# A cross-attention, attention and mixture-of-experts layer on one core: a sixth gate/up product ahead of the gate, and twelve split down products

## The chip, the cores and the metric

One core of a Trainium2 chip. The time is device microseconds of the whole program, from one launch. The profile is of one execution; its engines are TensorE (PE, with its weight loads as PEld), VectorE (DVE), ScalarE (ACT), GpSimd (POOL) and SyncE (SP), which issues the transfers.

## What is computed

The input x is 4 x 32 rows of 256 (T = 128 tokens, which fill the 128 partitions). Three blocks follow one another, each on a layer norm of x and added to x:

```
x = x + xattn(layernorm(x), ctx_512)        # 16 heads, causal, keys from ctx[:, :32] (causal mask)
x = x + attn(layernorm(x))                  # 16 heads, each projection with a LoRA of rank 16
x = x + ffn(layernorm(x))

def ffn(flat):                              # D = 256, I = 128, E = 32 experts, K = 4
    scores = sqrt(softplus(flat @ router_w.T))
    idx = top_k(scores + expert_bias, 4);  p = normalised scores of these, else 0
    for each expert e:
        g = clip(flat @ gate_w[e].T, -7, 7);  u = clip(flat @ up_w[e].T, -7, 7)
        out += p[:, e] * ((silu(g) * u) @ down_w[e].T)
    out += the same with a shared expert, without p
```

All 32 experts are computed for all 128 tokens; the gate p is zero for most.

## The kernel before

Each engine has its own list of instructions, written out by hand, and runs it in order; semaphores tie the lists together (`wait_ge`, `then_inc`). Nothing is reordered by a scheduler, so the place of an instruction in its list matters.

**Units.** The experts are worked on in PAIRS = 16 pairs. Pair index p counts from 0; unit n = p + 1 is the work on it, and unit 0 is the shared expert. A unit goes through these steps:

- TensorE, `gate_up(n)` (L580): the gate and up products of both experts into one PSUM bank of 512 columns.
- VectorE, `clip(n)` (L957 on): bank to `gu_clip`.
- ScalarE, `silu_unit(n)` (L785): SiLU of the gate halves, written back into the bank.
- VectorE, `gate_h(n)` (L1010): SiLU times up times routing weight, into `h`.
- TensorE, `transpose_h(n)` (L596): h is transposed into a PSUM bank (`bHT`, two in turn).
- ScalarE, `hT_unit(n)` (L793): bank to `hT` or `hT_parts`. For split downs VectorE, `hT_low(n)` (L1029), subtracts to get the low half.
- TensorE, `down(n)` (L608): the down product, added up in bank bY.

**Split weights.** The weights come from memory as 32-bit floats into `gu_raw` (RAW = 8 slots) and `dn_w`. A product on them as they are is a slow one. So weights are split in a rounded high part and a low part, and three faster matmuls (high x high, high x low, low x high) take the place of one. For pairs 2 to 15, ScalarE writes the high part of the gate/up weights (`gu_high`, `gu_high_chunk` for a half, L693 and L700) and GpSimd the low one (`gu_low`, two tiles of 128 x 512 per pair), into `gu_w` with SLOTS = 7 slots. The cast of pair p >= 9 waits until the product whose slot it overwrites is done (`gu_ready`): that of pair 9 for the third product. The first WHOLE = 2 pairs are multiplied whole. The last LAST = 11 down products are split in the same way: `dn_high(i)` on ScalarE, `dn_low(i)` on GpSimd (one tile each), the first FIRST = 5 are whole. From i = 3 on the split down weights lie in slots of `gu_w` that gate/up products have left.

**Orders.** GpSimd: the low halves of pairs 2 to 15 in order, with the inverse root of the third variance ahead of pair 7, a down tile after each of pairs 12 to 15, then the remaining down tiles. TensorE: products 1 (with the shared expert and the logits in between) to 5, transposes 0 and 1, then for n = 2 to 16 product n + 4, transpose n, down n - 2, and the last two downs. The last down goes to a bank of its own (`bLast`) and waits for the last GpSimd tile. There are five banks for products (`bGU`), so product n waits for the gating of unit n - 5. VectorE: the routing, then gating 0, gating 1, clips 2 and 3, then for each n gating n, clip n + 2 and the low part of hT. ScalarE: SiLU n + 2, the cast of pair 10 + n, the copy of hT n, and the down casts due. The lines of ScalarE between the routing and the loop are these:

```
nc.scalar.activation(root[:], half_power[:], ACT.Exp, scale=0.5).then_inc(root_ready, 1)
nc.scalar.preload_act_table(ACT.Silu)
...
gu_high_chunk(WHOLE + 7, 0)
silu_unit(0)
silu_unit(1)
gu_high_chunk(WHOLE + 7, 1)
gu_high(EARLY)
silu_unit(2)
```

The end: ScalarE copies the low sums of bY (L825), VectorE adds them (L1043), then adds the last down (L1046), and the output is stored.

Of the kernel before, what the change touches and what calls it, by code (L numbers as in the profile page):

```python
# [38 lines left out]
WHOLE = 2  # L39
EARLY = 10  # L40
LAST = 11
# [18 lines left out]
def gu_slot(p):  # L60
    return (p - WHOLE) % SLOTS

# [9 lines left out]
def build(nc, x, consts, mask, small, ctx_kv, x_wq, lora, rows, attn_w, shared_w, moe_w, out):  # L72
    with ExitStack() as ctx:
# [107 lines left out]
        bGU = (bP[0][:, 0], bP[0][:, 1], bP[1][:, 0], bP[1][:, 1], bE)  # L181
# [196 lines left out]
        def _(pe):  # L378
# [196 lines left out]
            def gate_up_whole(n, k):  # L575

                return nc.tensor.matmul(bGU[n % 5][:, 0:GU], xfT[:, k, :], gu_raw[:, raw_slot(n - 1), k * GU:(k + 1) * GU],
                                        start=(k == 0), stop=(k == DC - 1))

            def gate_up(n):  # L580

                if n > 5:
                    pe.wait_ge(h_ready, n - 4)
                for k in range(DC):
                    if n <= WHOLE:
                        pe.wait_ge(ld_gu[n - 1], 16)
                        last = gate_up_whole(n, k)
                    else:
                        pe.wait_ge(gu_lo_ready[k], n - WHOLE)
                        for a, w in HI_LO:  # L590
                            last = nc.tensor.matmul(bGU[n % 5][:, 0:GU], xnT_parts[:, a, k, :],  # L591
                                                    gu_w[:, gu_slot(n - 1), w, k * GU:(k + 1) * GU],
                                                    start=(k == 0 and a == w == 0), stop=(k == DC - 1 and a == 1))
                last.then_inc(gu_ready, 1)

            def transpose_h(n, width=2):  # L596
                pe.wait_ge(h_ready, n + 1)
                if n >= 2:
                    pe.wait_ge(hT_ready, n - 1)
                if n - 2 > FIRST:  # L600
                    pe.wait_ge(hT_low_ready, n - 2 - FIRST)
                for e in range(width):
                    last = nc.tensor.transpose(bHT[n % 2][:, e * T:(e + 1) * T], h[:, n % 4, e, :], ident)  # L603
                last.then_inc(hT_psum, 1)

            def down(n):
# [8 lines left out]
                else:  # L615
# [3 lines left out]
                    if n == PAIRS:  # L619
                        pe.wait_ge(h_ready, PAIRS)  # L620
# [27 lines left out]
            for n in range(WHOLE + 1, 6):  # L648
                gate_up(n)
            transpose_h(0, width=1)  # L650
            transpose_h(1)
            for n in range(2, PAIRS + 1):
                if n + 4 <= PAIRS:
                    gate_up(n + 4)
                transpose_h(n)
                if n == 2:
                    pe.wait_ge(ln_step, 3)
                    nc.tensor.matmul(bY[:, 0:D], hT[:, 0, 0, :], shared_sb[:, DC * SHARED:], start=False, stop=False,
                                     skip_group_check=True).then_inc(y_done, 1)
                else:  # L660
                    down(n - 2)
# [4 lines left out]
        def _(act):  # L666
# [74 lines left out]
            for c in range(DC):  # L741
                gu_high_chunk(WHOLE + 2, c)
# [3 lines left out]
            gu_high(WHOLE + 3)  # L746
# [5 lines left out]
            copy_probsT(1)  # L752
            gu_high(WHOLE + 4)
# [28 lines left out]
            nc.scalar.activation(root[:], half_power[:], ACT.Exp, scale=0.5).then_inc(root_ready, 1)  # L782
            nc.scalar.preload_act_table(ACT.Silu)

            def silu_unit(n):  # L785
                act.wait_ge(clip_ready, n + 1)
                width = 2 if n else 1
                bank = bGU[n % 5] if n else bShared
                dst = bank[:, 0:width * 2 * I].rearrange("p (e w i) -> p e w i", e=width, w=2)[:, :, 0, :]
# [3 lines left out]
            def hT_unit(n, width=2):  # L793
                act.wait_ge(hT_psum, n + 1)
                dst = hT[:, n % 3, 0:width] if n <= FIRST else hT_parts[:, n % 3, 0]
                nc.scalar.activation(dst, bHT[n % 2][:, 0:width * T], ACT.Copy).then_inc(hT_ready, 1)  # L796
# [9 lines left out]
            gu_high_chunk(WHOLE + 7, 0)  # L806
            silu_unit(0)
            silu_unit(1)
            gu_high_chunk(WHOLE + 7, 1)
            gu_high(EARLY)  # L810
            silu_unit(2)
            hT_unit(0, width=1)
            for n in range(1, PAIRS + 1):
# [7 lines left out]
                for i in range(UNITS, LAST):  # L821
                    if dn_from(i) + 1 == n + 4:
# [5 lines left out]
        def _(dve):  # L828
# [126 lines left out]
            def clip(n):  # L955
                width = 2 if n else 1
                bank = bGU[n % 5] if n else bShared  # L957
# [18 lines left out]
            step(nc.vector.tensor_scalar(logits_n, bLogits, rstd[:, 2:3], None, ALU.mult))  # L976
            dve.wait_ge(one_plus_ready, 1)
# [19 lines left out]
            dve.wait_ge(zeroed, 3)  # L997
            step(nc.vector.tensor_copy(score2[:, E:E + 1], leftover[:]))
# [11 lines left out]
            def gate_h(n):  # L1010

                dve.wait_ge(silu_ready, n + 1)
                if n >= 4:
                    dve.wait_ge(hT_psum, n - 3)
                bank = bGU[n % 5] if n else bShared
                for e in range(2 if n else 1):
                    weight_e = gate[:, (n - 1) * 2 + e:(n - 1) * 2 + e + 1] if n else rstd[:, 2:3]
                    last = nc.vector.scalar_tensor_tensor(h[:, n % 4, e], gu_clip[:, n % 4, e, 1, :], weight_e,  # L1018
                                                          bank[:, e * 2 * I:e * 2 * I + I], ALU.mult, ALU.mult)
# [9 lines left out]
            def hT_low(n):  # L1029
                dve.wait_ge(hT_ready, n + 1)  # L1030
                nc.vector.tensor_tensor(hT_parts[:, n % 3, 1], bHT[n % 2][:, 0:2 * T].rearrange("p (e t) -> p e t", e=2),  # L1031
# [79 lines left out]
```

## Time and profile before

| what | us |
|---|---|
| median of three runs | 73.18 |
| the three runs | 72.33, 73.18, 77.66 |
| the profiled execution, its own time | 72.22 |
| its span, first to last instruction | 70.4 |
| TensorE busy in the span | 65.3 (93%) |
| GpSimd busy in the span | 54.2 (77%) |
| VectorE, ScalarE busy | 47.0, 46.0 |

The span is shorter than the time by what lies before the first and after the last instruction, 1.8 us here. The granted clock of TensorE was full in the whole span. Matmuls overlap one another in the records, so a group's duration is some 0.15 us longer than what it adds to the queue; in the chain of waits the overlap is taken out.

### The profile page before, as it was taken

What the parts mean: (1) busy time and instruction counts of PE and PEld (TensorE: products, weight loads), DVE (VectorE), ACT (ScalarE), POOL (GpSimd) and SP (SyncE); (2) the same over time, 40 slices, a digit from 0 to 9 for tenths busy, and PEclk for the clock granted to TensorE, in tenths of its full rate; (3) what the DMA queues carried; (4) which work ended last, traced back from release to release, by engine and by line L of the source; (5) the groups of instructions that cost most, each with busy time, mean ns of one, the idle gap of its engine ahead of it and who ended that gap; (6) DMA issues with size and microseconds to landing.
All of it is one profiled execution on the core that took longest, in us unless ns stands there. A gap on an engine that the chain in (4) does not pass through costs nothing.

```text
span 70.4 us, 1578 instructions
## 1 busy us (share of the span) xinstructions
PE 65.3 (93%) x542; PEld 48.5 (69%) x542; DVE 47.0 (67%) x133; ACT 46.0 (65%) x101; POOL 54.2 (77%) x60
## 2 busy tenths in 40 slices
PE   5999989999799999999989999999999999999940
PEld 2348647789564496467666878888887888788820
DVE  0089488486497536499999945679955887697440
ACT  0606375876998654769979899999668851275220
POOL 7430003889999996998799999999999999999000
PEclk9999999999999999999999999999999999999999
DMA  0998999999999999999999995200000000000002
GB/s 3 271 297 245 329 425 404 291 328 419 417 419 403 393 401 407 396 383 388 393 407 400 391 372 201 76 0 0 0 9 0 0 0 0 0 0 0 0 0 74
DMA packets 6343, 15.75 MB, mean 224 GB/s; under 512 B 704, under 2 KB 1472, under 8 KB 6336
## 3 DMA queue, kind: packets, MB, share of 16 engines
q1 hardware_dynamic: 6048, 15.39, 59.2%
q10 hardware_dynamic: 288, 0.27, 1.1%
q8 instruction: 4, 0.07, 0.4%
q14 instruction: 3, 0.02, 0.1%
HBM read 15.52 MB, written 0.13 MB: 222 GB/s over the span
## 4 chain that ended last, share of the span: by engine, by line
PE 52%; DMA 16%; DVE 14%; SPq 7%; ACT 4%; issue 3%; DVEq 0%; ACTq 0%
DMA gu_raw<-moe_w_dram 16%; PE bP L591 16%; PE bY L624 7%; PE bY L613 6%; PE bXT L603 5%; SPq L275 4%; PE bE L591 4%; DVE gu_clip L964 4%; PE bY L626 3%; SPq L283 2%; DVE h L1018 2%; PE bP L419 2%; PE bXT L448 1%; PE bXT L641 1%; PE bY L444 1%
## 5 line engine op out<-in xcount | busy, mean ns | idle before, releaser
L349 POOL TENSOR_TENSOR gu_w<-gu_raw,gu_w 128x512 fp32r<-128x512 f32 x27 | 33.7, 1277 | 0.6 <-ACT gu_w L705 0.6
L591 PE MATMUL bP<-gu_w,xnT_parts 128*128 128x512 f32 x66 | 18.6, 417 | 0.0
L591 PEld LDWEIGHTS bP<-gu_w,xnT_parts 128*128 128x128 f32 x66 | 12.2, 188 | 2.9 <-issue 0.5
L1018 DVE SCALAR_TENSOR_TENSOR h<-gu_clip,gate,bP 128x128 f32<-128x128 f32 x26 | 7.8, 344 | 5.2 <-ACT bP L790 5.2
L964 DVE TENSOR_SCALAR gu_clip<-bP,clip_at 128x512 f32<-128x512 f32 x13 | 10.4, 806 | 1.1 <-PE bP L591 1.1
L355 POOL TENSOR_TENSOR gu_w<-dn_w,gu_w 128x512 fp32r<-128x512 f32 x8 | 10.1, 1285 | 0.0
L698 ACT ACTIVATE gu_w<-gu_raw 128x1024 fp32r<-128x1024 f32 x9 | 9.4, 1048 | 0.3 <-issue 0.3
L796 ACT ACTIVATE hT_parts<-bXT 128x256 fp32r<-128x256 f32 x11 | 4.2, 383 | 7.1 <-PE bXT L603 7.1
L705 ACT ACTIVATE gu_w<-gu_raw 128x512 fp32r<-128x512 f32 x10 | 6.1, 621 | 1.2 <-DMA gu_raw<-moe_w_dram 1.2
L603 PE MATMUL bXT<-consts_sb,h 128*128 128x128 f32 x33 | 6.5, 277 | 0.3 <-DVE h L1018 0.2
L790 ACT ACTIVATE bP<-gu_clip,rstd 128x256 f32<-128x256 f32 x13 | 6.1, 472 | 0.4 <-DVE gu_clip L964 0.4
L603 PEld LDWEIGHTS bXT<-consts_sb,h 128*128 128x128 f32 x33 | 4.4, 140 | 2.8 <-DVE h L1018 1.2
L339 POOL TENSOR_TENSOR aw_sb<-aw_sb,lora_v 128x256 f32<-128x256 f32 x2 | 1.4, 728 | 6.3 <-DMA aw_sb<-attn_w_dram 6.3
L624 PE MATMUL bY<-gu_w,hT_parts 128*128 128x512 f32 x14 | 5.7, 433 | 0.0
L1031 DVE TENSOR_TENSOR hT_parts<-bXT,hT_parts 128x256 fp32r<-128x256 f32 x11 | 4.6, 418 | 1.0 <-ACT hT_parts L796 1.0
L455 PE MATMUL bE<-const-bfloat16-1.0 128*128 128x512 bf16 x12 | 4.5, 516 | 0.8 <-PEq L1104 0.8
L613 PE MATMUL bY<-dn_w,hT 128*128 128x256 f32 x20 | 5.1, 380 | 0.0
L591 PE MATMUL bE<-gu_w,xnT_parts 128*128 128x512 f32 x18 | 4.9, 407 | 0.0
L803 ACT ACTIVATE gu_w<-dn_w 128x512 fp32r<-128x512 f32 x8 | 4.6, 623 | 0.0
L331 POOL TENSOR_TENSOR rstd<-var_eps,inv_sqrt_power 128x1 f32<-128x1 f32 x3 | 1.8, 598 | 3.0 <-DVE var_eps L842 3.0
L626 PE MATMUL bY<-gu_w,hT_parts 128*128 128x256 f32 x14 | 3.9, 281 | 0.0
L355 POOL TENSOR_TENSOR dn_first<-dn_w,dn_first 128x512 fp32r<-128x512 f32 x3 | 3.8, 1282 | 0.0
(161 smaller groups left out, 124.8 us busy)
## 6 DMA issues: line engine op xcount, KB each, us to landing
gu_raw<-moe_w_dram SPq DMA_DIRECT2D x16, 512.0 KB, 9.6
dn_w<-moe_w_dram SPq DMA_DIRECT2D x16, 256.0 KB, 9.5
aw_sb<-attn_w_dram SPq DMA_DIRECT2D x2, 512.0 KB, 7.4
shared_sb<-shared_w_dram SPq DMA_DIRECT2D x1, 416.0 KB, 14.9
small_sb<-small_dram SPq DMA_DIRECT2D x1, 338.0 KB, 7.3
xwq_sb<-x_wq_dram SPq DMA_DIRECT2D x1, 256.0 KB, 3.5
lora_sb<-lora_dram SPq DMA_DIRECT2D x1, 256.0 KB, 4.7
ctx_sb<-ctx_kv_dram ACTq DMA_DIRECT2D x1, 192.0 KB, 3.2
```

What stands on the lines that cost most here:

```text
L349: nc.gpsimd.tensor_tensor(gu_w[:, gu_slot(p), 1, cols], gu_raw[:, raw_slot(p), cols], gu_w[:, gu_slot(p), 0, cols], ALU.subtract).then_inc ...
L355: nc.gpsimd.tensor_tensor(dn_parts(i)[:, 1], dn_w[:, at:at + 2 * D], dn_parts(i)[:, 0], ALU.subtract).then_inc(dn_lo_ready, 1)
L591: last = nc.tensor.matmul(bGU[n % 5][:, 0:GU], xnT_parts[:, a, k, :], gu_w[:, gu_slot(n - 1), w, k * GU:(k + 1) * GU], start=(k == 0 and a ...
L603: last = nc.tensor.transpose(bHT[n % 2][:, e * T:(e + 1) * T], h[:, n % 4, e, :], ident)
L613: last = nc.tensor.matmul(bY[:, 0:D], hT[:, n % 3, e, :], dn_w[:, at:at + D], start=False, stop=False, skip_group_check=True)
L624: nc.tensor.matmul(bY.rearrange("p (w n) -> p w n", w=2), hT_parts[:, n % 3, 0, e, :], parts, start=False, stop=False, skip_group_check=True)
L626: last = nc.tensor.matmul(bY[:, 0:D], hT_parts[:, n % 3, 1, e, :], parts[:, 0], start=False, stop=False, skip_group_check=True)
L698: nc.scalar.activation(gu_w[:, gu_slot(p), 0], gu_raw[:, raw_slot(p)], ACT.Copy).then_inc(gu_hi_ready, DC)
L705: nc.scalar.activation(gu_w[:, gu_slot(p), 0, cols], gu_raw[:, raw_slot(p), cols], ACT.Copy).then_inc(gu_hi_ready, 1)
L790: nc.scalar.activation(dst, gu_clip[:, n % 4, 0:width, 0, :], ACT.Silu, scale=rstd[:, 2:3]).then_inc(silu_ready, 1)
L964: nc.vector.tensor_scalar(gu_clip[:, n % 4, 0:width], bank[:, 0:width * 2 * I], clip_at[:, 0:1], clip_at[:, 1:2], ALU.min, ALU.max).then_i ...
L1018: last = nc.vector.scalar_tensor_tensor(h[:, n % 4, e], gu_clip[:, n % 4, e, 1, :], weight_e, bank[:, e * 2 * I:e * 2 * I + I], ALU.mult, ...
```

## The change

- BANKS = 6: the sixth product goes once to a sixth bank (bXT1), ahead of transpose 0; product 7 goes ahead of transpose 1, and in the loop product n + 6 (was n + 4) ahead of transpose n. From then on five banks in turn. `LEADS` is empty, so the lead stays to the end.
- Transposes up to 6 all go to bXT0, one after another; later ones alternate as before. The routing's scratch moves from bXT1 to free columns of the bank bXT0, and the SiLU of unit 0 goes to the bank of unit 1, so both gatings wait for both SiLUs.
- LAST = 12: down 5 is split as well; GpSimd and ScalarE get one tile more. The down casts from i = 3 on are issued when `ahead(n)` passes them, two iterations earlier than before.
- ScalarE: in the second attention the query chunks are written ahead of the casts of pair 4; the cast of pair 5 is halved and its second half goes behind the copy of the probabilities; the whole cast of pair 9 goes ahead of the load of the SiLU table; that of pair 10 is halved.
- VectorE: the copy of the leftover column moves to an earlier place of the routing.

```diff
-LAST = 11
+BANKS = 6
+LEADS = ()
+LAST = 12
+def ahead(n):
+    return min(n + BANKS - sum(n >= at for at in LEADS), PAIRS)
...
-        logits_n, den, inv_root = (bXT1[:, at:at + E] for at in (64, 128, 192))
-        score2, weight = (bXT1[:, at:at + E + 1] for at in (256, 320))
-        bHT = (bXT1, bXT0)
+        logits_n, den, inv_root = (bShared[:, at:at + E] for at in (288, 320, 352))
+        score2, weight = (bShared[:, at:at + E + 1] for at in (384, 448))
+        bOnce = bXT1
+        def bGU(n):
+            if n == BANKS:
+                return bOnce
+            return (bP[0][:, 0], bP[0][:, 1], bP[1][:, 0], bP[1][:, 1], bE)[(n if n < BANKS else n - 1) % 5]
+        def bHT(n):
+            return bXT0 if n <= BANKS or n % 2 == 0 else bXT1
...
             def gate_up(n):
-                if n > 5:
-                    pe.wait_ge(h_ready, n - 4)
+                if n > BANKS:
+                    pe.wait_ge(h_ready, n - BANKS + (1 if n < 2 * BANKS else 2))
...
             def transpose_h(n, width=2):
                 pe.wait_ge(h_ready, n + 1)
-                if n >= 2:
-                    pe.wait_ge(hT_ready, n - 1)
-                if n - 2 > FIRST:
-                    pe.wait_ge(hT_low_ready, n - 2 - FIRST)
+                back = 1 if n <= BANKS else 2
+                if n >= back:
+                    pe.wait_ge(hT_ready, n - back + 1)
+                if n - back > FIRST:
+                    pe.wait_ge(hT_low_ready, n - back - FIRST)
...
-            for n in range(WHOLE + 1, 6):
+            for n in range(WHOLE + 1, BANKS + 1):
                 gate_up(n)
             transpose_h(0, width=1)
+            gate_up(BANKS + 1)
             transpose_h(1)
             for n in range(2, PAIRS + 1):
-                if n + 4 <= PAIRS:
-                    gate_up(n + 4)
+                if ahead(n) > ahead(n - 1):
+                    gate_up(ahead(n))
                 transpose_h(n)
...
             for c in range(DC):
-                gu_high_chunk(WHOLE + 2, c)
                 act.wait_ge(q_psum, DC + c + 1)
                 nc.scalar.activation(qT[:, 1, c], bP[c][:, 1, 0:T], ACT.Identity,
                                      bias=small_sb[:, BIASQ + c:BIASQ + c + 1]).then_inc(q_ready, 1)
-            gu_high(WHOLE + 3)
+                gu_high_chunk(WHOLE + 2, c)
+            gu_high_chunk(WHOLE + 3, 0)
...
             copy_probsT(1)
+            gu_high_chunk(WHOLE + 3, 1)
             gu_high(WHOLE + 4)
...
+            gu_high(WHOLE + 7)
             nc.scalar.preload_act_table(ACT.Silu)
             def silu_unit(n):
-                act.wait_ge(clip_ready, n + 1)
+                act.wait_ge(clip_ready, max(n, 1) + 1)
...
-            gu_high_chunk(WHOLE + 7, 0)
             silu_unit(0)
             silu_unit(1)
-            gu_high_chunk(WHOLE + 7, 1)
-            gu_high(EARLY)
+            for c in range(DC):
+                gu_high_chunk(EARLY, c)
             silu_unit(2)
...
                 for i in range(UNITS, LAST):
-                    if dn_from(i) + 1 == n + 4:
+                    if ahead(n - 1) <= dn_from(i) < ahead(n):
                         dn_high(i)
...
             step(nc.vector.tensor_scalar(logits_n, bLogits, rstd[:, 2:3], None, ALU.mult))
+            dve.wait_ge(zeroed, 3)
+            step(nc.vector.tensor_copy(score2[:, E:E + 1], leftover[:]))
             dve.wait_ge(one_plus_ready, 1)
...
             step(nc.vector.tensor_tensor(inv_root, inv_root, softplus[:], ALU.mult))
-            dve.wait_ge(zeroed, 3)
-            step(nc.vector.tensor_copy(score2[:, E:E + 1], leftover[:]))
...
             def gate_h(n):
-                dve.wait_ge(silu_ready, n + 1)
+                dve.wait_ge(silu_ready, max(n, 1) + 1)
```

## Rows read from the trace of the kernel before

**Rows 1.** The page's first part: busy us, share of the span, instructions.

```profile
PE 65.3 (93%) x542; PEld 48.5 (69%) x542; DVE 47.0 (67%) x133; ACT 46.0 (65%) x101; POOL 54.2 (77%) x60
```

**Rows 2.** Stretches: start and end, length, busy us of PE, PEld, DVE, ACT, POOL.

```profile
38.00:50.00 12.00, 12.00 (x60) 9.96 (x59) 8.99 (x23) 10.97 (x22) 12.00 (x10) 1.00 0.47 176
50.00:60.00 10.00, 10.00 (x52) 8.24 (x52) 7.23 (x17) 6.63 (x16) 10.00 (x9) 1.00 0.01 2
```

**Rows 3.** GpSimd in order of time: start, us, instruction [idle before it, and its releaser].

```profile
27.59 0.68 POOL L331 TENSOR_TENSOR rstd<-var_eps,inv_sqrt_power 128x1 f32<-128x1 f32 x1 [0.59 <-DVE var_eps L842]
28.24 5.00 POOL L349 TENSOR_TENSOR gu_w<-gu_raw,gu_w 128x512 fp32r<-128x512 f32 x4
33.83 10.00 POOL L349 TENSOR_TENSOR gu_w<-gu_raw,gu_w 128x512 fp32r<-128x512 f32 x8 [0.60 <-ACT gu_w L705]
55.03 10.05 POOL L355 TENSOR_TENSOR gu_w<-dn_w,gu_w 128x512 fp32r<-128x512 f32 x8
```

**Rows 4.** TensorE in order of time, 18 to 38 us, and its last down.

```profile
18.65 0.45 PE L419 MATMUL bP<-k_heads,qT 64*32 64x128 f32 x16 [0.36 <-ACT qT L744]
...
30.47 1.96 PE L591 MATMUL bP<-gu_w,xnT_parts 128*128 128x512 f32 x6
...
35.10 0.33 PE L603 MATMUL bXT<-consts_sb,h 128*128 128x128 f32 x1
35.62 0.44 PE L603 MATMUL bXT<-consts_sb,h 128*128 128x128 f32 x2 [0.19 <-DVE h L1018]
35.81 1.65 PE L591 MATMUL bP<-gu_w,xnT_parts 128*128 128x512 f32 x6
37.57 0.44 PE L603 MATMUL bXT<-consts_sb,h 128*128 128x128 f32 x2
...
66.75 0.87 PE L630 MATMUL bP<-gu_w,hT_parts 128*128 128x256 f32 x6
```

**Rows 5.** The chain of waits: start, us, what was on it.

```profile
17.71 0.63 ACT gu_w L705
...
32.80 0.17 DVE bXT L998
...
66.95 0.39 ACT y_low L825
...
67.83 0.42 DVE x_sb L1046
```

**Rows 6.** ScalarE in order of time.

```profile
24.13 0.37 ACT L755 ACTIVATE heads_outT<-bP,small_sb 128x128 f32<-128x128 f32 x1 [0.59 <-PE bP L440]
...
31.83 1.28 ACT L783 ACT_TABLE_LOAD   x1
...
33.66 0.35 ACT L790 ACTIVATE bXT<-gu_clip,rstd 128x128 f32<-128x128 f32 x1
33.95 0.46 ACT L790 ACTIVATE bP<-gu_clip,rstd 128x256 f32<-128x256 f32 x1
...
37.03 0.48 ACT L790 ACTIVATE bP<-gu_clip,rstd 128x256 f32<-128x256 f32 x1
37.45 1.04 ACT L698 ACTIVATE gu_w<-gu_raw 128x1024 fp32r<-128x1024 f32 x1
...
47.81 1.14 ACT L803 ACTIVATE gu_w<-dn_w 128x512 fp32r<-128x512 f32 x2
```

**Rows 7.** VectorE in order of time: the first gating.

```profile
34.70 0.34 DVE L1018 SCALAR_TENSOR_TENSOR h<-gu_clip,rstd,bXT 128x128 f32<-128x128 f32 x1
```

**Rows 8.** The chain again: a product, a whole down, the halves of a split one.

```profile
38.44 1.40 PE bP L591 x6
...
40.06 0.86 PE bY L613 x4
...
52.46 0.24 PE bY L624
52.70 0.12 PE bY L626
```

More of the change, by code:

```diff
@@ L590, in gate_up @@
                         for a, w in HI_LO:
-                            last = nc.tensor.matmul(bGU[n % 5][:, 0:GU], xnT_parts[:, a, k, :],
+                            last = nc.tensor.matmul(bGU(n)[:, 0:GU], xnT_parts[:, a, k, :],
                                                     gu_w[:, gu_slot(n - 1), w, k * GU:(k + 1) * GU],
@@ L597, in transpose_h @@
                 pe.wait_ge(h_ready, n + 1)
-                if n >= 2:
-                    pe.wait_ge(hT_ready, n - 1)
-                if n - 2 > FIRST:
-                    pe.wait_ge(hT_low_ready, n - 2 - FIRST)
+                back = 1 if n <= BANKS else 2
[3 more added lines that the diff above has]
+                    pe.wait_ge(hT_low_ready, n - back - FIRST)
                 for e in range(width):
-                    last = nc.tensor.transpose(bHT[n % 2][:, e * T:(e + 1) * T], h[:, n % 4, e, :], ident)
+                    last = nc.tensor.transpose(bHT(n)[:, e * T:(e + 1) * T], h[:, n % 4, e, :], ident)
                 last.then_inc(hT_psum, 1)
@@ L782, in _ @@
             nc.scalar.activation(root[:], half_power[:], ACT.Exp, scale=0.5).then_inc(root_ready, 1)
+            gu_high(WHOLE + 7)
             nc.scalar.preload_act_table(ACT.Silu)
             def silu_unit(n):
-                act.wait_ge(clip_ready, n + 1)
+                act.wait_ge(clip_ready, max(n, 1) + 1)
                 width = 2 if n else 1
-                bank = bGU[n % 5] if n else bShared
-                dst = bank[:, 0:width * 2 * I].rearrange("p (e w i) -> p e w i", e=width, w=2)[:, :, 0, :]
+                dst = bGU(max(n, 1))[:].rearrange("p (e w i) -> p e w i", e=2, w=2)
+                dst = dst[:, :, 0, :] if n else dst[:, 0:1, 1, :]
                 nc.scalar.activation(dst, gu_clip[:, n % 4, 0:width, 0, :], ACT.Silu, scale=rstd[:, 2:3]
@@ L956, in clip @@
                 width = 2 if n else 1
-                bank = bGU[n % 5] if n else bShared
+                bank = bGU(n) if n else bShared
                 if n:
@@ L1010, in gate_h @@
             def gate_h(n):
-                dve.wait_ge(silu_ready, n + 1)
+                dve.wait_ge(silu_ready, max(n, 1) + 1)
                 if n >= 4:
                     dve.wait_ge(hT_psum, n - 3)
-                bank = bGU[n % 5] if n else bShared
+                bank = bGU(max(n, 1))
+                at = 0 if n else I
                 for e in range(2 if n else 1):
@@ L1018, in gate_h @@
                     last = nc.vector.scalar_tensor_tensor(h[:, n % 4, e], gu_clip[:, n % 4, e, 1, :], weight_e,
[L1019 removed]
+                                                          bank[:, at + e * 2 * I:at + e * 2 * I + I], ALU.mult, ALU.mult)
                 last.then_inc(h_ready, 1)
```

9 lines of the change are left out of this document (4 added, 5 removed).

## The prediction

> **What bounds the kernel now.** I read the shares of the engines first, then the stretches, then the chain of waits, and then the queues of GpSimd, TensorE, ScalarE and VectorE in order of time. The shares show TensorE busy 93% and GpSimd 77% [rows 1], an average over stages that differ. By stretch, both are full from 38 us on: 12.00 and 10.00 us of 12 and 10 on either engine [rows 2]. GpSimd works without a gap from 33.83 us to 65.08 us (55.03 + 10.05) [rows 3], 25 tiles of 1.25 us, each tile the low half of 512 columns. TensorE runs products, transposes and downs from 37.57 us on with no wait of any kind. So the second half has one engine on the chain and a second one just behind it: the low half of the last down was ready at 65.08 us, and TensorE came to that down at about 66.80 us [rows 3, 4]. GpSimd's margin is 1.7 us. That is the number on which the change has to be judged, because it moves TensorE earlier and gives GpSimd one tile more.
>
> Ahead of that the chain goes through ScalarE's cast of pair 4 (17.71 us, waiting for its transfer), the query, attention, and then the routing on VectorE to the gate [rows 5]. The profiled execution took 72.22 us for a span of 70.4 us, 1.8 us around it. The median shown is 73.18 us, its lowest run 72.33 us: the profiled run stands at the lower end, and two runs of the same kernel lie 0.85 us apart. About 2% (1.45 us) is what a measurement of this kernel can tell from no change.
>
> **Queries ahead of the casts.** TensorE sat idle 0.36 us before the scores of the second attention, until query chunk 0 was there [rows 4]; that chunk stood behind the cast that waited for its transfer and then took 0.63 us [rows 5]. With the query first, it is ready before the projections end. Late next are those projections themselves, so at most 0.36 us is gained; I take 0.34 us (a handoff costs 0.02 us). The low end is 0, if something else of attention is just as late. The cast of pair 5 is halved and its second half moved behind the copy of the probabilities; ScalarE has a gap of 0.59 us there [rows 6] and GpSimd needs that half 0.6 us later, so it is at no cost. One cover gone would cost a cast of 0.6 us. Everything behind attention thus starts 0.34 us earlier, on all engines.
>
> **The copy of the leftover column** leaves the routing, where it held 0.17 us and a link of 0.02 to 0.03 us [rows 5], for a gap in which VectorE waits for ScalarE: 0.2 us off the routing. By both, the gate would be ready 0.54 us earlier. Moving the routing's scratch from one PSUM bank to another leaves each instruction as it is: 0.
>
> **Cast 9 ahead of the SiLU table.** This is where I expect the gain of the gate to be lost. Before, the table load came right behind the root (31.83 us, 1.28 us), and the first half of the cast after it [rows 6]. Now the whole cast (1.04 us, as that of pair 11 [rows 6]) stands ahead of the load, and it waits for the third product, whose slot it overwrites. That product ended at 30.47 + 1.96 = 32.43 us [rows 4], or 32.09 us with the 0.34 us. ScalarE is free at 31.47 us, so it waits 0.6 us. Cast 32.11 to 33.14 us; load to 34.43 us; SiLU of unit 0 to 34.73 us (its slot of 33.66 to 33.95 us was 0.29 us); SiLU of unit 1, 0.46 us, to 35.20 us. Before it ended at 34.41 us [rows 6], just ahead of VectorE's first gating at 34.70 us [rows 7]. The first gating now waits for the SiLU of unit 1 too (unit 0 is written into unit 1's bank). It starts at 35.2 us, 0.5 us later than before, though the gate itself is ready at 34.2 us. Bounds: no delay at all (34.2 us) if the slot is free at once, 35.55 us if the queries bring nothing.
>
> **GpSimd's line.** Behind the first gating the order is fixed: gating 0, gating 1, clips 2 and 3, SiLU of unit 3, cast of pair 11, and that is what GpSimd needs next. Before: first gating 34.70 us, SiLU 37.03 us, cast 37.45 us, end 38.49 us [rows 6, 7]; GpSimd came to pair 11 at 33.83 + 4 x 1.25 = 38.83 us [rows 3], so it never saw it. After: the cast ends at 38.49 + 0.5 = 39.0 us. GpSimd would be there at 38.2 us: its waits for the third variance and for pair 9, 0.59 and 0.60 us [rows 3], shrink (pair 9 is cast at 33.14 us instead of 33.73 us). It waits 0.8 us and starts pair 11 at 39.0 us. From there 10 gate/up tiles and 12 down tiles in place of 11: 22 x 1.25 = 27.5 us, end at 66.5 us, against 65.08 us before. Nothing hides the twelfth tile.
>
> A rule of the Trainium skill speaks against the change here. The page Perfetto Trace Analysis, section Identifying the Most-Contended Engine, says to judge TensorE by its weight loads and not by its matmuls, and to optimize first the engine with the highest occupancy. By that this is GpSimd, at 77% against 69% of weight loads [rows 1], and the change adds to it. Were that all, the end would move by the tile of 1.25 us less the 1.7 us of margin, which is nothing; the rule comes true only because TensorE moves earlier as well.
>
> **TensorE's line.** From the end of product 5 (35.10 us) it idled 0.41 us ahead of transpose 1 and 0.32 us ahead of transpose 2 [rows 4]. Product 6 now fills that: 1.40 us of work [rows 8] moved to where the gate was awaited, of which only the 0.73 us of idle time can be gained. Down 5 goes from four whole matmuls, 0.86 us, to split ones, 0.24 + 0.12 + 0.23 + 0.12 = 0.71 us [rows 8]: 0.15 us less. Added waits: product n+6 waits for the gated unit n+1 (before, product n+4 for unit n), and transposes 1 to 6 share one bank, so each waits for ScalarE's copy of the one before. Laid out by the durations of the rows, the copies come 0.1 to 1 us ahead. Three products wait: product 8 for unit 2 (VectorE is 0.5 us late), 0.2 us; products 12 and 13 for units 7 and 8, 0.2 us each, since ScalarE has two down casts (1.14 us for the two [rows 6]) ahead of the SiLU at an earlier iteration. Behind such a waiting product stand a transpose and a down; nobody else needs them sooner, as VectorE and ScalarE are then themselves the late ones. Sum: 66.80 - 0.34 - 0.15 - 0.73 + 0.6 = 66.2 us at the last down; bounds 65.5 us (no wait, all of it) and 68 us (the slow rival).
>
> **The sum.** The last down needs both lines, GpSimd at 66.5 us and TensorE at 66.2 us; GpSimd is later. Then 0.03 us, the six matmuls of 0.87 us [rows 4], 0.05 us: the last add starts at 67.5 us instead of 67.83 us [rows 5]. (The other branch, the copy of the low sums from 66.95 us on, then gives 67.3 us.) That is 0.3 us less: 71.9 us against the profiled 72.22 us. The middle one of the three near runs (72.22, 72.33, 73.18) less 0.3 us gives 72.0 us, which I take.
>
> **Rivals.** (1) GpSimd is fed in time: the third product frees its slot early enough, or SiLU 1 isn't what holds the first gating. For it: at most 0.6 us of wait has to go. Against: the wait is in the queue's order. GpSimd then ends at 65.4 to 65.8 us, and TensorE decides, with 65.6 to 66.1 us at the last down: the last add starts at 66.7 to 67.0 us, 0.8 to 1.1 us less than before, 71.3 us. (2) Slower: ScalarE's queue in iterations 4 to 8. Two down casts per iteration are now issued two iterations earlier, among them while the casts of pairs 14 and 15 still run, ahead of the SiLU for which the next product waits. In the stretch 38 to 50 us ScalarE was busy 10.97 of 12 us [rows 2]. I find 0.2 us of wait at two products; if each of five products waits 0.5 us, TensorE comes to the last down at 68.1 us, the last add starts at 69.1 us, 1.2 us later than before: 73.4 us. It decides once the waits of TensorE from 38 to 60 us exceed 1.3 us in all. (3) The reorder does nothing and the slot is late: without the 0.34 us, cast 11 ends at 39.35 us, GpSimd at 66.85 us, and the time stays at 72.2 us.
>
> **How the numbers follow.** Forecast 0.46, rival 1 0.26, rival 2 0.16, rival 3 0.12. The range takes in rivals 1 and 3 whole and rival 2 up to 73.2 us, which leaves some 0.15 out, the far part of rival 2 and a gain over 1.3 us: 70.9 to 73.2 us. No case but a gain that I haven't found, or one run against another, reaches 2% below: 0.12. Rival 2 reaches 2% above in its worse half: 0.08. The rest, 0.80, is within 2%.
>
> **What the profile after would show.** The gap of 0.36 us before the scores gone, attention's end 0.34 us earlier. A wait of about 0.6 us on ScalarE ahead of cast 9, the table load at 33.15 us, the first gating at 35.2 us though the gate was ready near 34.2 us. GpSimd idle 0.7 to 0.8 us ahead of pair 11 and its last tile ending at 66.5 us. TensorE without the two gaps at 35 to 37.5 us, and a wait of 0.2 to 0.4 us directly ahead of the last down, released by GpSimd. Wrong would prove me: TensorE waiting for gated units more than twice beyond 40 us (rival 2), or the last tile of GpSimd in before TensorE asks (rival 1).

## The result

The changed kernel is slower: 73.49 us median against 72.64 us, ratio 1.0108, 95% interval 1.0078 to 1.0137, that is 0.8 us more. I had forecast 0.3 us less, 72.0 us, with a range to 73.2 us. Some executions of either kernel begin late or with a lowered clock; the ratios leave them out, and the rows below are of a second, undisturbed execution of the changed kernel (72.97 us, run e1).

The page of the profile after, against [rows 1]:

```profile
span 71.2 us, 1582 instructions
...
PE 66.3 (93%) x542; PEld 48.2 (68%) x542; DVE 47.4 (67%) x134; ACT 47.0 (66%) x103; POOL 55.6 (78%) x61
```

TensorE in order of time, the answer to [rows 4]: the projections and scores of the second attention; product 6, transpose 0, product 7, transpose 1, product 8; whole downs (L631) with products 11, 12 and 13 behind them; product 16; transposes 11 to 14; the last down.

```profile
16.74 1.95 PE L409 MATMUL bP<-xnT,aw_sb 128*128 128x128 f32 x16
18.62 0.45 PE L436 MATMUL bP<-k_heads,qT 64*32 64x128 f32 x16
...
35.05 1.57 PE L608 MATMUL bXT<-gu_w,xnT_parts 128*128 128x512 f32 x6
36.46 0.27 PE L621 MATMUL bXT<-consts_sb,h 128*128 128x128 f32 x1
36.63 1.67 PE L608 MATMUL bP<-gu_w,xnT_parts 128*128 128x512 f32 x6
38.15 0.41 PE L621 MATMUL bXT<-consts_sb,h 128*128 128x128 f32 x2
38.58 1.66 PE L608 MATMUL bP<-gu_w,xnT_parts 128*128 128x512 f32 x6
...
44.81 1.03 PE L631 MATMUL bY<-dn_w,hT 128*128 128x256 f32 x4
45.49 1.74 PE L608 MATMUL bP<-gu_w,xnT_parts 128*128 128x512 f32 x6
...
47.29 1.03 PE L631 MATMUL bY<-dn_w,hT 128*128 128x256 f32 x4
48.28 1.67 PE L608 MATMUL bP<-gu_w,xnT_parts 128*128 128x512 f32 x6
...
50.01 1.03 PE L631 MATMUL bY<-dn_w,hT 128*128 128x256 f32 x4
50.94 1.67 PE L608 MATMUL bP<-gu_w,xnT_parts 128*128 128x512 f32 x6
...
58.04 1.57 PE L608 MATMUL bP<-gu_w,xnT_parts 128*128 128x512 f32 x6
...
60.38 0.38 PE L621 MATMUL bXT<-consts_sb,h 128*128 128x128 f32 x2
...
61.31 0.38 PE L621 MATMUL bXT<-consts_sb,h 128*128 128x128 f32 x2
...
62.46 0.41 PE L621 MATMUL bXT<-consts_sb,h 128*128 128x128 f32 x2
...
64.03 0.41 PE L621 MATMUL bXT<-consts_sb,h 128*128 128x128 f32 x2 [0.45 <-DVE hT_parts L1052]
...
67.54 0.87 PE L648 MATMUL bP<-gu_w,hT_parts 128*128 128x256 f32 x6
```

Product 11 follows its down after 0.68 us, products 12 and 13 after 0.99 and 0.93 us: waits of 0.31 and 0.25 us. Product 16 is out at 59.45 us, and what is left for TensorE is a transpose and a split down per iteration. Undisturbed, such an iteration takes 61.31 - 60.38 = 0.93 us. But transpose 13 follows 1.15 us after transpose 12, and transpose 14 follows 1.57 us after 13: waits of 0.2 and 0.65 us. The releaser of the second is VectorE's low part: transpose 14 goes to the bank of transpose 12, so it waits until the low part of unit 12 has been read out of it.

VectorE's first gating, the gating that product 12 waited for, and then the stretch of the tail, gating (L1039), clip (L984), low part (L1052) by turns:

```profile
35.71 0.35 DVE L1039 SCALAR_TENSOR_TENSOR h<-gu_clip,rstd,bP 128x128 f32<-128x128 f32 x1 [1.35 <-ACT bP L811]
...
47.62 0.61 DVE L1039 SCALAR_TENSOR_TENSOR h<-gu_clip,gate,bP 128x128 f32<-128x128 f32 x2 [1.85 <-ACT bP L811]
...
60.29 0.42 DVE L1052 TENSOR_TENSOR hT_parts<-bXT,hT_parts 128x256 fp32r<-128x256 f32 x1 [0.63 <-ACT hT_parts L817]
60.66 0.60 DVE L1039 SCALAR_TENSOR_TENSOR h<-gu_clip,gate,bP 128x128 f32<-128x128 f32 x2
61.18 0.80 DVE L984 TENSOR_SCALAR gu_clip<-bE,clip_at 128x512 f32<-128x512 f32 x1
61.90 0.41 DVE L1052 TENSOR_TENSOR hT_parts<-bXT,hT_parts 128x256 fp32r<-128x256 f32 x1
62.23 0.59 DVE L1039 SCALAR_TENSOR_TENSOR h<-gu_clip,gate,bP 128x128 f32<-128x128 f32 x2
62.75 0.80 DVE L984 TENSOR_SCALAR gu_clip<-bP,clip_at 128x512 f32<-128x512 f32 x1
63.47 0.41 DVE L1052 TENSOR_TENSOR hT_parts<-bXT,hT_parts 128x256 fp32r<-128x256 f32 x1
63.80 0.59 DVE L1039 SCALAR_TENSOR_TENSOR h<-gu_clip,gate,bE 128x128 f32<-128x128 f32 x2
```

From gating to gating it takes 62.23 - 60.66 = 1.57 us, without a gap, as long as there is a clip in the turn. It had waited 0.63 us just before, for the copy of transpose 10, which TensorE had put behind product 16. The low part of unit 12 is the one at 63.47 us; it stands in VectorE's list behind gating 14 (62.23 us) and the clip of unit 16 (62.75 us).

ScalarE and GpSimd, as [rows 6] and [rows 3], two views:

```profile
31.36 0.23 ACT L802 ACTIVATE root<-half_power 128x32 f32<-128x32 f32 x1 [0.26 <-DVE half_power L1013]
32.53 1.06 ACT L717 ACTIVATE gu_w<-gu_raw 128x1024 fp32r<-128x1024 f32 x1 [0.94 <-PE bP L608]
33.61 1.28 ACT L804 ACT_TABLE_LOAD   x1
34.91 0.77 ACT L811 ACTIVATE bP<-gu_clip,rstd 128x128 f32<-128x128 f32 x2
```

```profile
33.67 5.17 POOL L366 TENSOR_TENSOR gu_w<-gu_raw,gu_w 128x512 fp32r<-128x512 f32 x4 [0.44 <-ACT gu_w L717]
39.58 5.04 POOL L366 TENSOR_TENSOR gu_w<-gu_raw,gu_w 128x512 fp32r<-128x512 f32 x4 [0.74 <-ACT gu_w L717]
...
55.80 11.31 POOL L372 TENSOR_TENSOR gu_w<-dn_w,gu_w 128x512 fp32r<-128x512 f32 x9
```

Both waits are where the forecast had them, with 0.6 and 0.8 us: the cast waits 0.94 us for the third product, and GpSimd waits 0.74 us for pair 11 and ends at 67.11 us. The last down starts 0.43 us after that. So GpSimd is not what it waited for.

### The profile page after: what moved, and what is told of

It is laid out like the page before. It is cut to its first block, busy times and chain, and to the rows that moved or that the text cites. A ratio compares the mean times of both kernels' runs of the same rounds, so it can differ in the third digit from the quotient of the medians.

```text
span 75.5 us, 1580 instructions
## 1 busy us (share of the span) xinstructions
PE 70.8 (94%) x540; PEld 51.7 (68%) x542; DVE 47.5 (63%) x134; ACT 47.0 (62%) x103; POOL 55.7 (74%) x61
## 4 chain that ended last, share of the span: by engine, by line
PE 83%; DVE 8%; issue 3%; ACT 2%; DVEq 0%
PE bP L608 20%; PE bE L472 6%; PE bE L608 6%; PE bP L409 5%; PE bY L631 5%; PE bP L594 5%; PE bY L642 4%; PE bXT L621 4%; PE bP L436 3%; PE bXT L401 3%; PE bY L461 3%; PE bY L644 2%; PE bP L450 2%; PE bP L443 2%; PE bXT L608 2%
## 5 line engine op out<-in xcount | busy, mean ns | idle before, releaser
L608 PE MATMUL bP<-gu_w,xnT_parts 128*128 128x512 f32 x60 | 16.8, 415 | 0.0
L608 PEld LDWEIGHTS bP<-gu_w,xnT_parts 128*128 128x128 f32 x60 | 10.8, 188 | 3.7 <-DVE h L1039 1.2
L372 POOL TENSOR_TENSOR gu_w<-dn_w,gu_w 128x512 fp32r<-128x512 f32 x9 | 11.3, 1338 | 0.0
L984 DVE TENSOR_SCALAR gu_clip<-bP,clip_at 128x512 f32<-128x512 f32 x12 | 9.6, 805 | 0.0
L1039 DVE SCALAR_TENSOR_TENSOR h<-gu_clip,gate,bP 128x128 f32<-128x128 f32 x24 | 7.2, 344 | 3.7 <-ACT bP L811 3.4
L717 ACT ACTIVATE gu_w<-gu_raw 128x1024 fp32r<-128x1024 f32 x8 | 8.4, 1052 | 1.0 <-PE bP L608 1.0
L724 ACT ACTIVATE gu_w<-gu_raw 128x512 fp32r<-128x512 f32 x12 | 7.0, 619 | 0.0
L811 ACT ACTIVATE bP<-gu_clip,rstd 128x256 f32<-128x256 f32 (+1 forms) x13 | 6.0, 466 | 0.9 <-DVE gu_clip L984 0.9
L642 PE MATMUL bY<-gu_w,hT_parts 128*128 128x512 f32 x16 | 6.5, 433 | 0.0
L1052 DVE TENSOR_TENSOR hT_parts<-bXT,hT_parts 128x256 fp32r<-128x256 f32 x12 | 5.0, 420 | 1.5 <-ACT hT_parts L817 1.4
L631 PE MATMUL bY<-dn_w,hT 128*128 128x256 f32 x16 | 4.1, 380 | 0.0
L608 PEld LDWEIGHTS bE<-gu_w,xnT_parts 128*128 128x128 f32 x18 | 3.3, 188 | 0.7
```

Source lines behind the costliest of these rows:

```text
L372: nc.gpsimd.tensor_tensor(dn_parts(i)[:, 1], dn_w[:, at:at + 2 * D], dn_parts(i)[:, 0], ALU.subtract).then_inc(dn_lo_ready, 1)
L608: last = nc.tensor.matmul(bGU(n)[:, 0:GU], xnT_parts[:, a, k, :], gu_w[:, gu_slot(n - 1), w, k * GU:(k + 1) * GU], start=(k == 0 and a == ...
L631: last = nc.tensor.matmul(bY[:, 0:D], hT[:, n % 3, e, :], dn_w[:, at:at + D], start=False, stop=False, skip_group_check=True)
L642: nc.tensor.matmul(bY.rearrange("p (w n) -> p w n", w=2), hT_parts[:, n % 3, 0, e, :], parts, start=False, stop=False, skip_group_check=True)
L717: nc.scalar.activation(gu_w[:, gu_slot(p), 0], gu_raw[:, raw_slot(p)], ACT.Copy).then_inc(gu_hi_ready, DC)
L724: nc.scalar.activation(gu_w[:, gu_slot(p), 0, cols], gu_raw[:, raw_slot(p), cols], ACT.Copy).then_inc(gu_hi_ready, 1)
```

## The experiments

All runs are given by their ratio to the kernel before and, from the profile, by the start of the last down counted from the start of the projections of the second attention (e1: 67.54 - 16.74 = 50.80 us). This second number (the frame, below) leaves out what an execution's beginning adds: the projections began anywhere from 16.34 to 21.06 us in these profiles, but the two of the changed kernel give 50.74 and 50.80 us, and b1, e5 and e12, all with the order of the kernel before on TensorE, 49.92 to 49.98 us. It does not leave out waits on transfers, which come at other times in each execution (e6 and e7).

| run | kernel | ratio, 95% interval | last down after projections, us |
|---|---|---|---|
| before, first profile | | 1 | 50.41 |
| b1 | before again | | 49.92 |
| after | changed, first profile | 1.0108, 1.0078 to 1.0137 | 50.74 |
| e1 | changed again | 1.012, 1.0075 to 1.0165 | 50.80 |
| e2 | lead falls to four | 1.0038, 0.9989 to 1.0088 | 50.39 |
| e3, e14 | eleven downs | 1.0146, 1.0079 to 1.0212; 1.0148, 1.0088 to 1.0207 | 51.32 (e14) |
| e4 | table first | 1.0111, 1.004 to 1.0182 | 50.02 |
| e13 | table first, transfers | 1.0025, 0.999 to 1.0059 | 50.06 |
| e5 | before with the queries' edit | 1.0018, 0.9968 to 1.0068 | 49.92 |
| e12 | before with the transfers' edit | 1.0054, 1.0006 to 1.0101 | 49.98 |
| e6 | lead falls, table first | 0.996, 0.9903 to 1.0017 | 49.57 |
| e7 | e6 with eleven | 0.9947, 0.9888 to 1.0006 | 50.70 |
| e8 | changed, half clips 15 and 16 | 1.0097, 1.0048 to 1.0146 | 50.37 |
| e9 | table first, eleven, lead kept | 1.0113, 1.0073 to 1.0153 | 50.20 |
| e10 | e7 with the transfers' edit | 0.9882, 0.9823 to 0.9941 | 49.30 |
| e11 | e6 with the transfers' edit | 0.9897, 0.9833 to 0.9961 | 49.39 |

**e1: the changed kernel again.** No edit.

> The changed kernel again, for an undisturbed profile. Theory A (the tail on VectorE): in the profile at hand the six transpose-and-down iterations that follow product 16 take 0.92 us each on TensorE while VectorE's gating, clip and low part take 1.57 us, and TensorE waits 0.2 and 0.6 us for VectorE ahead of transposes 13 and 14; the last down is then 0.3 to 0.4 us after GpSimd's last tile. Theory B (GpSimd alone): no wait on VectorE, the last down directly behind GpSimd's last tile. Measured from the start of the projections of the second attention, A gives the last down 50.7 us later, B 50.4 us, the kernel before had 50.4 us. The ratio to before stays near 1.01; what the frame does not explain (0.4 us or so) must then lie ahead of the projections.

Theory A: 50.80 us, the waits are there, GpSimd's last tile is 0.43 us early. But the ratio asks for 0.8 us, and against the 50.41 us of the first profile of before the frame gave only 0.4 us.

**b1: the kernel before again.** No edit.

> The kernel before once more, for a second profile. Its first profile began the projections of the second attention at 16.34 us, those of four kernels with the same code up to there at 16.74 us and later. If that is chance of an execution (the nine warm-up matmuls took 3.48 us there and 3.8 to 4.0 us in the others), this one lies at 16.7 us or so too. Then the wait of 0.36 us before the scores, which ended with the transfer of pair 4 at 17.7 us plus a cast, is 0 to 0.1 us here, since the transfer lands at the same absolute time: the gain of the query edit is then mostly not there in a usual execution. If the wait is still 0.3 us or more, the query edit gains always.

TensorE of the kernel before in this execution; in [rows 4] the scores had come 2.31 us after the projections began (at 16.34 us), with 0.36 us idle:

```profile
17.21 1.95 PE L392 MATMUL bP<-xnT,aw_sb 128*128 128x128 f32 x16
19.09 0.45 PE L419 MATMUL bP<-k_heads,qT 64*32 64x128 f32 x16
...
67.13 0.87 PE L630 MATMUL bP<-gu_w,hT_parts 128*128 128x256 f32 x6
```

Here they come 1.88 us after them, with no wait, just as in the changed kernel (18.62 - 16.74 = 1.88 us). The gap that the query edit removes is there only when attention comes early against the transfer; this execution's began 0.9 us later, and the transfer of pair 4 had landed by then. (That it lands at the same time in every execution was an assumption; e6 and e7 show another one that does not.) The kernel before thus needs 49.92 us in the frame, and the changed one 0.88 us more, which is the measured 0.8 us.

**e5: the queries alone.**

```diff
 # the kernel before
             for c in range(DC):
-                gu_high_chunk(WHOLE + 2, c)
                 act.wait_ge(q_psum, DC + c + 1)
                 nc.scalar.activation(qT[:, 1, c], ...)
-            gu_high(WHOLE + 3)
+                gu_high_chunk(WHOLE + 2, c)
+            gu_high_chunk(WHOLE + 3, 0)
...
             copy_probsT(1)
+            gu_high_chunk(WHOLE + 3, 1)
             gu_high(WHOLE + 4)
```

> The kernel before with the query chunks ahead of the casts of pair 4 and the cast of pair 5 in two halves, alone. If the query edit gains in every execution: 0.3 us less, ratio 0.995 to 0.996. If it only gains where attention comes early relative to the transfer: ratio 0.998 to 1.001.

1.0018, a little above the second case; the interval leaves out the 0.3 us of the first one. In its profile the scores come 1.88 us after the projections, as in b1. No gain that can be measured.

**e2: the lead falls.**

```diff
-LEADS = ()
+LEADS = (9, 10)
```

> The changed kernel with the lead falling from six to four at iterations 9 and 10 (LEADS = (9, 10)), so that products 15 and 16 stand between late transposes as before. Theory A: VectorE gets products' time to finish its clips among them, the waits ahead of transposes 13 and 14 go, 0.3 to 0.6 us less than the changed kernel, until GpSimd's last tile is the bound. Theory B: no change, GpSimd's line is untouched. A third possibility: the waits only move to iterations 9 and 10, no change either, with VectorE's waits seen there.

0.6 us less by the ratios, whose intervals just overlap, 0.41 us by the frame. TensorE's waits for VectorE ahead of transposes 13 and 14 are gone; what it waits for now is GpSimd. From the view of who waited for whom, 36 to 68 us, of e2:

```profile
PEld bY L642 <- POOL gu_w L372: 0.4, 1, 0.4
PEld bP L648 <- POOL gu_w L372: 0.3, 1, 0.3
```

The first is ahead of down 8, at 57.29 us; the second is ahead of the last down, which starts at 67.30 us, just behind the end of GpSimd's last tile at 67.24 us. So in the changed kernel GpSimd and TensorE's tail lay 0.4 us apart, and the tail was the later one. With the lead falling, iterations 9 and 10 are transposes and downs only, and products 15 and 16 stand behind them; the transposes come sooner, and with them the copies and low parts that VectorE's list waits for.

**e8: half of two clips.** It leaves out the clip of the second expert in units 15 and 16.

```diff
             def clip(n):
-                width = 2 if n else 1
+                width = 2 if 0 < n < PAIRS - 1 else 1
```

> The changed kernel with the clips of units 15 and 16 on their first expert alone (the second expert's halves of both are left unclipped and stale), which takes some 0.35 us each off VectorE in the tail and nothing off any other engine; the order stays. Theory A: the waits of 0.2 and 0.6 us ahead of transposes 13 and 14 shrink or go, the last down comes earlier until GpSimd's last tile (67.14 us against 67.54 us) holds it: 0.3 to 0.4 us less than the changed kernel. Theory B: nothing.

```profile
63.07 0.54 DVE L984 TENSOR_SCALAR gu_clip<-bE,clip_at 128x256 f32<-128x256 f32 x1
...
65.38 0.41 PE L621 MATMUL bXT<-consts_sb,h 128*128 128x128 f32 x2 [0.17 <-DVE hT_parts L1052]
```

Each of the two clips takes 0.54 us in place of 0.80 us. Taking these 0.5 us of work off VectorE and nothing off any other engine brings the last down 0.43 us forward in the frame (50.37 us). The wait ahead of transpose 13 is gone, the one ahead of transpose 14 shows as 0.17 us, and the last down now waits for GpSimd (0.3 us in the view of waits). This profile is of an execution that began late (projections at 18.69 us), but up to transpose 10 it lies within 0.1 us of e1 in the frame (42.65 against 42.71 us). By the ratio it is only 0.2 us less than e1, and the intervals overlap. Place and limit are as theory A has them; its size rests on this one profile.

**e3 and e14: eleven split downs.**

```diff
-LAST = 12
+LAST = 11
```

> The changed kernel with eleven split downs instead of twelve: one tile of 1.25 us less on GpSimd, one cast of 0.6 us less on ScalarE, one low part of 0.33 us less on VectorE, 0.15 us more on TensorE. Theory B: 0.6 to 1.1 us less than the changed kernel. Theory A: VectorE sets the tail, 0 to 0.4 us less. If both lie equally close: about 0.3 us.

> The changed kernel with eleven split downs again, whose first profile had a lowered clock. Expected: GpSimd's last tile comes 1.2 us earlier than in the changed kernel, the last down doesn't, since the waits on VectorE ahead of transposes 13 and 14 stay: ratio 1.010 to 1.014.

Theory B, and with it my forecast's mechanism, falls: GpSimd's last tile ends at 65.96 us in e14 (it began its last eight at 55.96 us), 1.1 us earlier than in e1 (1.4 us in the frame), while the last down starts later, at 68.27 us, 2.3 us behind it. Nothing of the 1.25 us comes back. The expected 1.010 to 1.014 was a little low: in this execution a wait of TensorE stood ahead of product 12, with ScalarE waiting ahead of the cast of pair 12 (views of TensorE and of ScalarE, e14):

```profile
48.88 1.67 PE L608 MATMUL bP<-gu_w,xnT_parts 128*128 128x512 f32 x6 [0.34 <-DVE h L1039]
```

```profile
40.67 1.06 ACT L717 ACTIVATE gu_w<-gu_raw 128x1024 fp32r<-128x1024 f32 x1 [0.34 <-issue]
```

**e4: the table first.**

```diff
             nc.scalar.activation(root[:], half_power[:], ACT.Exp, scale=0.5).then_inc(root_ready, 1)
-            gu_high(WHOLE + 7)
             nc.scalar.preload_act_table(ACT.Silu)
...
+            gu_high_chunk(WHOLE + 7, 0)
             silu_unit(0)
             silu_unit(1)
+            gu_high_chunk(WHOLE + 7, 1)
             for c in range(DC):
                 gu_high_chunk(EARLY, c)
```

> The changed kernel with the load of the SiLU table back in its place right behind the root, and the cast of pair 9 in halves around the first two SiLUs as before. Both theories: no wait of 1 us ahead of the cast, the first gating 1.0 to 1.4 us earlier. If the late gate costs the change its gain: 0.5 us or more less than the changed kernel. If TensorE has work until then (products 6 and 7) and GpSimd's last tile is the bound, the gain is only what pair 11 is cast earlier, 0.3 to 0.7 us.

The first gating comes 1.4 us earlier counted from the projections (35.17 - 17.61 = 17.56 us against 35.71 - 16.74 = 18.97 us), and the frame is 0.78 us shorter, but the ratio stays at 1.011 (four executions). One of the two misled.

**e6 and e7: lead falls and table first, with twelve and with eleven.** Both edits above together, and `LAST = 11`.

> The changed kernel with the lead falling to four at iterations 9 and 10 and the table load back in its place. Theory A (VectorE sets the tail of the changed kernel, GpSimd stands 0.4 us behind it): the tail's waits on VectorE go by the lead, GpSimd's last tile comes earlier by the earlier cast of pair 11; measured from the projections the last down comes 0.7 to 1.1 us earlier than in the changed kernel, ratio to before 0.995 to 1.001. If the table's place costs nothing (as its own run suggested): as with the lead alone, 1.004.

> As the one before, with eleven split downs. If GpSimd's last tile is by now what the last down waits for, one tile less gives up to 1.2 us, until TensorE's own line ends it: 0.3 to 0.6 us less than the run with twelve, ratio 0.990 to 0.995, faster than both kernels. If GpSimd is not the bound: 0.1 us more than with twelve, from the whole down on TensorE.

e6 comes to 0.996, as expected for a table whose place matters (1.2 us less than e1 in the frame, a little more than the 0.7 to 1.1 us expected). e7 comes to 0.9947, only 0.1 us less than e6, where 0.3 to 0.6 us less was expected if GpSimd were the bound. ScalarE stands still ahead of the cast of pair 12 in both profiles, 0.64 us in e6 (cast at 40.26 us) and 1.59 us in e7:

```profile
38.46 0.47 ACT L810 ACTIVATE bE<-gu_clip,rstd 128x256 f32<-128x256 f32 x1
40.53 1.06 ACT L717 ACTIVATE gu_w<-gu_raw 128x1024 fp32r<-128x1024 f32 x1 [1.59 <-issue]
```

The view names no releaser. The cast waits for the transfer of pair 12 and for product 6, which was done at 36.24 us, and the wait is gone once that transfer is issued earlier (e10, below). Its issue and its time to landing, in e1 and in e7 (view of the tile gu_raw on SyncE, 31.4 to 31.6 us in e1, 31.2 to 31.35 us in e7):

```profile
L300 SPq DMA_DIRECT2D gu_raw<-moe_w_dram x1: 378/378/378, 31.5 to 31.5; - x1
DMA to landing us min/median/max: 8.0/8.0/8.0
...
L300 SPq DMA_DIRECT2D gu_raw<-moe_w_dram x1: 377/377/377, 31.3 to 31.3; - x1
DMA to landing us min/median/max: 9.2/9.2/9.2
```

So it landed at 39.4 us in e1 and at 40.5 us in e7, just before the cast; the same view gives 39.6 us for e4, 40.2 us for e6 and 40.6 us for e14. The landing moves by 1.2 us from one execution to another, and not with the beginning of attention: e1 and e7 began within 0.2 us of each other (projections at 16.74 and 16.53 us). ScalarE does move with it. With the table first it is ready for the cast 22.4 us after the projections began: at 38.94 us in e7, at 39.62 us in e6, and at 39.98 us in e4, whose execution began late (17.61 us), whose transfer landed early, and which has no such wait. That e4's frame left out what a usual execution pays is argued from this; e13 below tests it.

**e9: the lead kept, all else as e7.**

```diff
-LEADS = (9, 10)
+LEADS = ()
```

> The changed kernel with the table load first and eleven split downs, but the lead kept at six to the end: the kernel of run e7 without its fall. Against e7 it isolates the lead. Theory A: VectorE's tail is all there, 0.4 to 0.8 us more than e7, ratio 1.000 to 1.006. If the lead's end is harmless once GpSimd and the table are out of the way: as e7, 0.995.

1.0113 against 0.9947: keeping the lead costs 1.2 us by the ratios, more than the 0.4 to 0.8 us expected, and the two intervals do not touch. The waits of 0.2 and 0.65 us ahead of transposes 13 and 14 are as in e1, which is 0.85 us, and against e10, whose profile has no wait for pair 12, the frame is 0.9 us longer. By their intervals the two ratios lie 0.5 to 1.9 us apart, so 0.9 us is within them.

**e10, e11 and e12: the transfers of pairs 12 and 13 ahead of those of 14 and 15,** in e7, in e6 and in the kernel before.

```diff
-            for p in range(2 * RAW - WHOLE, PAIRS):
-                load_gu(p)
-            for p in range(RAW + 4, 2 * RAW - WHOLE):
+            for p in range(RAW + 4, PAIRS):
                 load_gu(p)
```

> Run e7 (lead falls, table first, eleven) with the transfers of pairs 12 and 13 issued ahead of those of 14 and 15. In e7 ScalarE waited 1.59 us for pair 12 at 40.5 us, and TensorE 0.4 and 0.5 us and GpSimd 0.75 us behind it. If that wait counts, 0.3 to 0.7 us less than e7, ratio 0.985 to 0.991; if it only shows in an execution that begins early, 0.1 us or nothing.

> The same with twelve split downs (e6 with the transfers reordered). GpSimd's line is 1.25 us longer than in the run with eleven. If GpSimd is the last to arrive at the last down once all else is out of the way, 0.5 to 1.0 us more than with eleven, ratio 0.995; if TensorE's line is, 0.1 us less than with eleven.

> The kernel before with only the transfers of pairs 12 and 13 ahead of those of 14 and 15. In its profile ScalarE waited 0.35 us for pair 12 at 39.5 us and nothing behind it was late. So 0 to 0.1 us: ratio 0.998 to 1.001. If it is 0.99, the gain of the two fastest kernels is the transfers' order and not the earlier products.

e10 is faster than both kernels, 0.9882, 0.5 us less than e7, and its cast of pair 12 starts at 39.02 us without a wait. e11 comes to 0.9897: the twelfth tile costs nothing that can be measured, though its last down does wait for GpSimd (0.3 us). The control e12 has 1.0054, above the expected 0.998 to 1.001, and a frame of 49.98 us: the transfers' order gains nothing by itself, and may cost a little.

**e13: the table first with the transfers.**

> The changed kernel (lead kept, twelve) with the table load first and the transfers reordered. With the table first alone the time stayed at 1.011 though its profile, one that began late, had the last down 0.8 us earlier counted from the projections. If what was lacking is the transfer of pair 12, which a usual execution waits for once ScalarE is earlier, this one shows it: 0.5 us less than with the table first alone, ratio 1.002 to 1.005, the waits of 0.2 and 0.6 us on VectorE in the tail still there. If the ratio stays at 1.01, the table's place is worth nothing and the frame of the one profile misled.

1.0025, 0.6 us less than e4 (the intervals just overlap), in the expected range; the wait of 0.45 us on VectorE is still there at 63.90 us. Against the changed kernel the two edits together are worth 0.6 to 0.7 us by the ratios and 0.74 us in the frame, which TensorE gains back around product 7 and transpose 1 (0.5 us) and ahead of product 12 (0.3 us). With the control e12, this is the price of the table's place, once the transfer no longer takes the place of the wait removed. The transfers' edit was not tried alone on the changed kernel.

## Why the prediction was wrong

In the frame the forecast had the last down at 66.5 - 16.3 = 50.2 us, against 50.41 us in the one profile of before. It came at 50.80 us, and the kernel before usually needs 49.92 us. The first difference, 0.6 us, is TensorE's line; the second, 0.5 us, is the profile that the forecast started from. Together they are the 1.1 us between 0.3 us less and 0.8 us more.

**The query edit, taken at 0.34 us: 0 in a usual execution** (b1, e5). The term came from one profile, which happened to begin early; I bounded it below by 0 and then took the top. The price of a wait on a transfer depends on when it lands and when the waiting engine gets there, and the row said that this was one: the chain passed through the transfer of pair 4 at 17.7 us.

**"Three products wait ... 0.6 us" on TensorE's line: the step that failed.** Measured from the end of product 5, TensorE takes 67.54 - 35.05 = 32.49 us to the last down, for 30.7 us of work: 1.8 us of waits. (In b1 the same stretch takes 67.13 - 35.54 = 31.59 us, 0.7 us of it the waits ahead of transposes 1 and 2 that the change removes, and 0.15 us the whole down 5. So the change takes out 0.85 us, puts in 1.8 us, and the kernel is 0.9 us slower.) Of these 0.9 us lie in the head and ahead of products 12 and 13 (iterations 6 and 7), where I had laid out 0.6 us, and 0.85 us in the tail, where I had none. I had laid out the transposes' waits for ScalarE and the products' for the gating, and stopped with product 16, taking the last six iterations at 0.92 us each. VectorE needs 1.57 us for each that has a clip. The lead does not give VectorE any start: in its list the low part of unit n - 2 stands ahead of gating n + 1, and that low part waits for a transpose that the lead has put 2.75 us later (transpose 10 at 59.45 - 16.74 = 42.71 us, in b1 at 57.17 - 17.21 = 39.96 us). The lead's price is shown beyond the intervals by e9 against e7; that it is VectorE's work in the tail rests on the profiles of e1, e2 and e8. Not tried: the low part ahead of the clip in VectorE's list, or a third bank for the transposes.

**GpSimd's line: right.** The end at 66.5 us, 50.2 us after the projections, was measured as 50.37 us; waits for pair 9 and pair 11 0.44 and 0.74 us. What was wrong was that it sets the end: the last tile is in 0.43 us before TensorE asks for it, the sign that the forecast had named for rival 1, though here TensorE is late and not GpSimd early. It is second by 0.43 us, and becomes first once VectorE's tail is gone (e2, e8), but then TensorE's own line is hardly earlier. So taking the twelfth tile away gains nothing that can be measured (e14, and e10 against e11, 0.09 us in the frame).

**The cast ahead of the table: right in time** (wait 0.94 us, table at 33.61 us, first gating at 35.71 us; I had 0.6, 33.15 and 35.2 us, for an execution beginning 0.4 us sooner), and right that it costs something. Its price is 0.6 to 0.7 us (e13), but taken away alone it gains nothing by the ratio (e4), most likely because it uncovers the wait for pair 12. That wait stood in the profile of before, and the forecast did not follow it:

```profile
39.48 1.06 ACT L698 ACTIVATE gu_w<-gu_raw 128x1024 fp32r<-128x1024 f32 x1 [0.35 <-issue]
```


**The copy of the leftover column** was covered by the late SiLU, as said; it was not tried by itself. **Rival 2** had the sign, and part of the mechanism: products 12 and 13 do wait for units that are gated late, 0.31 and 0.25 us where I had 0.2 us each, and VectorE waits 1.85 us ahead of the gating at 47.62 us for a SiLU that stands behind three down casts in ScalarE's list. But that is far from its 0.5 us at each of five products; the larger single loss is VectorE in iterations 13 and 14.

The rule on the most contended engine (Trainium skill, Perfetto Trace Analysis, section Identifying the Most-Contended Engine) pointed at GpSimd, 78% busy in e1 against 68% of weight loads. For this tail the runs don't bear it out: removing a tile of GpSimd gains nothing (e14), removing work of VectorE, 67% busy, moves the last down in the profile (e8).

## What to carry to other kernels

When products are moved ahead of consumers, lay out the tail too: what the products used to hide there is the other engines' work per iteration, and the drain runs at the pace of the slowest one (1.57 us against 0.93 us here). An engine's share of the span does not show that. A wait on a transfer in one profile should be priced with a second profile, since both the waiting engine's time and the landing move from one execution to another, and not together (one transfer landed at 39.4 us in e1 and at 40.6 us in e14). And edits that release one wait each should be tried together: against the changed kernel the table's place gained 0.1 us alone and the lead's fall 0.6 us, and the transfers' order gained nothing on the kernel before, but the three together (e11) take 1.6 us off the changed kernel.

## What was not expected of the hardware

The nine warm-up matmuls at the start took 3.48 us in the first profile of the kernel before and 4.00 us in e1, with the same code. All of the first attention then lies some 0.4 us later. In e1 the same instruction adds 0.22 us each later in the program (two take 0.60 us, one 0.38 us), so the nine ran at half that speed. And in the executions whose attention began late (e5, e8, e9: projections at 18.7 to 19.0 us) the eight 128x128 matmuls of the first attention's query product took 2.06 to 2.08 us, against 1.15 us in e1. In the page's slices all of these have a full granted clock, so the profile shows the lower speed only in the durations, and does not say why.
